# A one-hot matrix scaled half on ScalarE and half on VectorE, in a graph-layer kernel whose gathers are issued by GpSimd

## The reference

```python
f0, f1 = fctp_scalar(x0, x1, node_attr, W_l1_0, W_l1_1, MUL)      # per node, 32 + 32x3
h = SILU_NORM * silu(edge_scalars @ (W_fc1 / 8.0))
weight = h @ (W_fc2 / 8.0)                                        # per edge, 4 x 32: wA, wC, wD, wB
g0, g1 = f0[edge_src], f1[edge_src]                               # the gather
e0, e1 = edge_attr[:, :1], edge_attr[:, 1:]                       # 4 numbers per edge
outA = wA * g0 * e0
outB = wB * einsum('euk,ek->eu', g1, e1) / SQRT3
outC = (wC * g0)[..., None] * e1[:, None, :]
outD = wD[..., None] * g1 * e0[..., None]
mA, mB, mC, mD = (segment_sum(v, edge_dst, num_segments=n) / 4 for v in (outA, outB, outC, outD))
```

## Time and profile before

| | us |
|---|---|
| median of 3 runs | 5603.18 (5603.14 to 5605.29) |
| the profiled execution, its own time | 5602.97 |
| its span | 5601.3 |
| busy: PE, DVE, ACT, POOL | 3539.7, 2754.8, 2524.7, 4131.5 |
| matmul weight loads (PEld) | 2936.4 |

### The profile page before, as it was taken

The page is one execution under the profiler, slowest core; times in us unless marked ns, Lnnn a source line. Parts: engine busy times, 40 slices in busy tenths (PEclk is TensorE's granted clock), DMA queues, the critical chain, the costliest instruction groups (busy, mean ns, idle before and its releaser), DMA issues. The chain is left out here.

```text
span 5601.3 us, 82999 instructions
## 1 busy us (share of the span) xinstructions
PE 3539.7 (63%) x18413; PEld 2936.4 (52%) x18413; DVE 2754.8 (49%) x11200; ACT 2524.7 (45%) x8901; POOL 4131.5 (74%) x3327
## 2 busy tenths in 40 slices
PE   1555555555545555555553566888888888888871
PEld 0443433433433434433342344888888888888861
DVE  2655656556555556555553455333333333333338
ACT  0222222222222222222221223888888888888860
POOL 0888888888888888888887434777777777777753
PEclk9776676776766777667676666777777777777765
DMA  8666666666666666666665663333333333333323
GB/s 221 124 110 114 114 111 117 110 116 111 111 116 111 113 116 109 119 110 110 119 110 78 151 147 94 81 80 81 80 81 80 81 80 81 80 79 80 80 75 117
DMA packets 748228, 588.04 MB, mean 105 GB/s; under 512 B 336912, under 2 KB 616361, under 8 KB 745112
## 3 DMA queue, kind: packets, MB, share of 16 engines
q0 software_dynamic: 286576, 224.93, 28.9%
q1 hardware_dynamic: 453266, 330.14, 21.5%
q10 hardware_dynamic: 8342, 32.53, 1.4%
HBM read 374.65 MB, written 212.60 MB: 105 GB/s over the span
## 5 line engine op out<-in xcount | busy, mean ns | idle before, releaser
L704 POOL DMA_INDIRECT sums_scratch<-vals,to_i x1568 | 2447.0, 1561 | 617.4 <-issue 514.7
L984 POOL DMA_INDIRECT fg<-f_scratch,src_e x1568 | 1492.0, 952 | 501.3 <-issue 477.5
L1037 ACT ACTIVATE hot<-raw,e_s 128x40 f32<-128x40 f32 x6272 | 1392.2, 313 | 355.7 <-DVE raw L1060 314.9
L618 PE MATMUL ps_n<-same,hot 128*40 128x128 f32 x3136 | 698.4, 416 | 1340.5 <-issue 1338.1
L618 PEld LDWEIGHTS ps_n<-same,hot 128*40 128x40 f32 x3136 | 559.9, 185 | 1448.3 <-issue 1385.0
L1013 PE MATMUL ps_eu<-hot,prod 128*128 128x120 f32 x3136 | 890.2, 378 | 0.0
L661 ACT COPY near<-ps_n 40x512 f32<-40x512 f32 x196 | 113.3, 578 | 1655.6 <-PE ps_n L618 1655.6
L1011 PEld LDWEIGHTS ps_eu<-hot,prod 128*128 128x128 f32 x3136 | 623.8, 244 | 308.1 <-DVE prod L1067 269.2
L1011 PE MATMUL ps_eu<-hot,prod 128*128 128x40 f32 x3136 | 619.7, 289 | 250.8 <-DVE prod L1067 250.3
L1066 DVE TENSOR_TENSOR prod<-ps_ew,fg 128x256 f32<-128x256 f32 x392 | 164.3, 419 | 1234.9 <-DMA fg<-f_scratch,src_e 1234.9
L1013 PEld LDWEIGHTS ps_eu<-hot,prod 128*128 128x128 f32 x3136 | 620.6, 246 | 0.0
(11 more groups left out here) (193 smaller groups left out, 3818.0 us busy)
## 6 DMA issues: line engine op xcount, KB each, us to landing
srow_s<-in_src SPq DMA_DIRECT2D x196, 512.0 KB, 3.5
e_s<-in_edge_attr SPq DMA_DIRECT2D x196, 256.0 KB, 3.8
hid_scratch<-hid SPq DMA_DIRECT2D x196, 256.0 KB, 3.8
hid_e<-hid_scratch SPq DMA_DIRECT2D x196, 256.0 KB
sums_scratch<-zeros ACTq DMA_DIRECT2D x24, 1056.0 KB, 26.2
sums_scratch<-vals,to_i POOLq DMA_INDIRECT x1568, 3.4
fg<-f_scratch,src_e POOLq DMA_INDIRECT x1568
t_in<-sums_scratch POOLq DMA_DIRECT2D x72, 256.0 KB, 5.7
```

The lines of the kernel that those rows point to most:

```text
L618: last = pe.matmul(ps_n[t // TH][:, t % TH, :], hot[:, k, t, :], same[:, k, t, :], start=True, stop=True)
L704: pool.indirect_dma_start(out=sums_d[i], out_offset=bass.IndirectOffsetOnAxis(ap=to_i[:, j, t:t + 1], axis=0), in_=vals[:, j, t, :], in_of ...
L984: pool.indirect_dma_start(out=fg[:, j, t, :], out_offset=None, in_=f_d, in_offset=bass.IndirectOffsetOnAxis(ap=src_s[:, j, t:t + 1], axis= ...
L1037: last = act.activation(hot[:, k, t, c, :], raw[:, k, t, :], ACT.Copy, scale=e4_s[:, j, t, c:c + 1])
```

## The change

Of the 8 tiles of the one-hot matrix only the first four (TH) are expanded by ACT in scaled copies. The other four are expanded by DVE in one product of 128 x (4 tiles x 4 attributes x 40), of `raw` broadcast over the attributes and `e4_s` broadcast over the 40 columns. It stands between `raw` and `prod` on DVE, with waits for the load of `e4_s`, for e_seg of super-group s - 2 (which read the `hot` slot) and for `raw`. It signals e_hot2, for which PE waits before the segment sum and SP before it loads a slot again.

```diff
@@ sync
                             done(sp, e_hot, s, UN)
+                            done(sp, e_hot2, s, UN)
                             done(sp, e_fc2, s, UN)
@@ tensor
                                 done(pe, e_hot, m)
+                                done(pe, e_hot2, m)
                                 done(pe, e_sums, m, 2)
@@ scalar
-                                for t in range(TS):
+                                for t in range(TH):
                                     for c in range(4):
                                         last = act.activation(hot[:, k, t, c, :], raw[:, k, t, :], ACT.Copy,
                                                               scale=e4_s[:, j, t, c:c + 1])
@@ vector
                                                   ALU.is_equal).then_inc(e_raw, 1)
+                                uses(dve, e4_ld[j], q + 1, 16)
+                                done(dve, e_seg, s, 2)
+                                done(dve, e_raw, s)
+                                dve.tensor_tensor(hot[:, k, TH:TS, :, :], raw[:, k, TH:TS, None, :].to_broadcast([P, TH, 4, W]),
+                                                  e4_s[:, j, TH:TS, :, None].to_broadcast([P, TH, 4, W]), ALU.mult).then_inc(e_hot2, 1)
                                 done(dve, e_fc2, s)
                                 uses(dve, gath[j], q + 1, 16 * TS)
```

More of the change, by code:

```diff
@@ L947, in graph_layers @@
             e_seg, e_sums, e_lin, e_add1, e_add = sem("e_seg"), sem("e_sums"), sem("e_lin"), sem("e_add1"), sem("e_add")
+            e_hot2 = sem("e_hot2")
             e_bases, clear_d = sem("e_bases"), sem("e_clear")
-            sems1 = src_ld + e4_ld + hid_ld + gath + [e_fc2, e_rel, e_raw, e_hot, e_prod,
+            sems1 = src_ld + e4_ld + hid_ld + gath + [e_hot2, e_fc2, e_rel, e_raw, e_hot, e_prod,
                                                       e_seg, e_sums, e_lin, e_add1, e_add, e_bases]
```

## The result

The changed kernel takes 5613.79 us (median of 20 runs, 5610.72 to 5617.96), the one before 5605.09 us (20 runs, 5600.15 to 5607.89). The ratio is 1.0017, 95% interval 1.001 to 1.0024: slower by 0.17%, 8.7 us, the interval reaches from some 6 to 13 us. In the profiled executions it is 5611.95 against 5602.97 us, and the span 5610.4 against 5601.3.

What follows compares the result with a forecast made beforehand. POOL's unpausing gathers were taken to bound the edge stage; gather delays of 4.8 and 8.2 us, about 0.1 for the others, less 0.7 now lost, made +13 us: 5603 + 13 = 5616 us, range 5601 to 5648.

Steps and rivals of the forecast that it cites:

- POOL sets the pace, and DVE's and ACT's work is hidden: Edge stage: POOL's gathers never pause, 1.257 us each; ACT's saved copies worth nothing, DVE's product hidden in 6.3 us idle.
- The product takes 0.83 us: DVE's new 128 x 640 product: 0.83 us from the line through `rel` and `raw`; bounds 0.49 and 0.947.
- A DVE operation with two SBUF inputs at a gather's start costs POOL its remainder less 0.13 us: Read from three long gathers, each with `raw` running at its start: 0.20, 0.15 and 0.32 us longer.
- The sum, +13 us: Gather delays in the edge stage: 4.8 plus 8.2 us plus about 0.1, less 0.7 already lost; 5616 us, +0.23%.
- the gap g: On DVE, from `raw`'s end to the product's start: 0.10 us; the sum would be 20 us at 0.06, 8 at 0.14.
- the 144 products of the middle phases: Super-groups whose `raw` starts 0.56 to 0.90 us after a gather: 13 products hold the next gather, 131 come behind its start.
- the term of 8.2 us: 13 products starting over 0.04 us before a gather hold it up by 0.63 us each.
- The other term: 42 super-groups with `raw` 0.00 to 0.27 us after a gather: product ends 0.24 us into the next, delaying it 0.11.
- the other super-groups: The 9 others: about 0.1 us lost together, less the 0.7 us that the three long gathers lose now.
- The first rival: Edge stage: the cover holds and the product delays no gather; 5603 us, not slower; chance 0.22.
- The third: A gather keeps DVE's two-input product out for its whole 0.95 us: 51 us more, 5667 us; chance 0.04.
- The second: The product starts earlier and wins nearly always, 144 x 0.65 = 94 us: at most about 5700; chance 0.13, including The third.

Runs made afterwards that it cites:

- ACT's relief alone: Changed kernel without the product: ACT expands 4 tiles, segment sums of tiles 4 to 7 reuse the matrix of tiles 0 to 3; 5604.29 us, ratio 0.9999.
- the reduce: Kernel before, ACT expanding all 8 tiles, plus a DVE sum over broadcast `raw` (one SBUF input) at the product's place; 5603.37 us, ratio 0.9998.
- the product behind prod: Changed kernel with the product and its three waits moved behind the last piece of `prod`; 5661.7 us, ratio 1.0107.
- six tiles: Changed kernel with 2 tiles on ACT and 6 on DVE, product 128 x 960; 5633.55 us, ratio 1.0043; on two other chips 0.9711 and 0.97.

## Why the prediction came out as it did

**POOL sets the pace, and DVE's and ACT's work is hidden**: right. ACT's relief alone is worth 0 (0.9999), and the reduce, as long as the product, costs 0 (0.9998). DVE's wait for gathers went from 1235 to 1054 us, where some 1050 were expected.

**The product takes 0.83 us**: right, 0.829.

**A DVE operation with two SBUF inputs at a gather's start costs POOL its remainder less 0.13 us**: right. Read from three rows, it held in 51 gathers of the changed kernel (0.09 to 0.13, median 0.127) and, as a calculation made beforehand, gave 60 us for the product behind prod (57 measured, with fewer collisions than expected) and 24 to 25 for six tiles (24.0).

**The sum, +13 us**: too large; the trace shows 7.9 and the runs 8.7. The step that failed in size is the gap g between `raw` and the product, taken as 0.10 us from `rel` to `raw`. It is 0.13 us (3506.44 + 0.49 to 3507.06), in 194 of 196 super-groups. In the trace of the kernel before, the gap from `rel` to `raw` isn't one value: 0.03 or 0.04 us in 102 super-groups, and 0.10 to 0.12 in 93. The product's wait for `raw` stands in an instruction of its own ahead of it. So does `raw`'s wait for `rel` where the loop turns, with 0.12 us in 47 super-groups; in the 102 `raw` carries the wait itself. That explains only part, since in 44 others, with the wait on `raw` too, the gap is 0.10. The prediction gives no reason for taking 0.10 and not the 0.03 that it also saw, which by its own working would have given over 20 us; in that the sum was lucky.

By the further 0.03 us, 3 of the 144 products of the middle phases would still start over 0.04 us before a gather instead of 13. In the trace of the changed kernel none held a gather up, and the term of 8.2 us became 0. The other term, 42 small collisions of 0.11 us or 4.8 us, grew to 43 of 0.16, 6.9 us, and of the other super-groups, taken at 0.1 us together, 7 cost 0.10 each. The forecast named 8 us for g = 0.14, but took 0.10 as the likeliest. That the time of 5616 us lies closer to 5613.79 than 13 to 8.7 comes from the median before, 5605.09 over all runs and not 5603.

With that the loss, 0.17%, lies in the range from 5601 to 5648 us, but just under the 0.2% which the forecast lay over and named as what can be told from no change. The first rival, no loss at all, was wrong: the interval begins at 1.001, and the trace shows the place of each lost tenth. The third, a gather that keeps DVE out for its whole length, was wrong too: the product stays at 0.829 us on average, and a `raw` that begins at a gather's start takes 0.53. The second, the product that wins nearly always, is in part what the product behind prod showed, where 91 of 137 won: right as a mechanism, in a place where the change doesn't put it.

## What to carry to other kernels

When GpSimd's gathers follow each other without a pause, ask of work that moves to VectorE not only whether it finds idle time, but whether it reads two SBUF tensors and where it lies against the starts of the gathers: the same product cost 8 or 57 us by its place, and an operation of the same length with one SBUF input nothing. Two or three longer-than-usual rows of an operation that is otherwise constant to 5 ns are worth looking at before one calls a cover free. Taking work from an engine that nobody waits for, busy 80% as ACT is here, brought nothing.

## What the runs showed of the hardware that I had not expected

On two of the chips the same kernel before took 6624 and 6558 us instead of 5605, nearly all of the difference in the gather stage: in the kernels with 8 gathers PE stood still some 800 to 1000 times for 0.3 to 2.5 us between matmuls for which nothing was missing that the profile shows. On the other chips that happened not once: the some 75 pauses of this length in the kernel before, which the last expectation sets beside them, were waits for `prod`. Six tiles on DVE were 3% faster than the kernel before on the two slower chips, against 0.4% slower elsewhere. What stops PE there, and why the time depends on the split there, was not found.

Which of the two goes first at a gather's start is decided within some 0.02 us: a `raw` that starts 0.04 us before the gather holds it (5302.56 in the earlier trace rows), one that starts 0.03 us before is itself held up by 0.07 us. So it is with a product. The one at 3686.62 above, 0.04 us before, holds the gather; in the changed kernel, at the same 0.04 us in the two decimals of the view, it is the product that is held up, to 0.90 us:

```profile
4071.27 0.90 DVE L1069 TENSOR_TENSOR hot<-raw,e_s 128x640 f32<-128x640 f32 x1
4071.31 0.95 POOL L986 DMA_INDIRECT fg<-f_scratch,src_e  x1 [0.30 <-issue]
```
